# Softmax and relu(h) of a graph network with slice attention worked in their PSUM banks, output stores on ScalarE, attention weights loaded earlier

## What is computed

```python
xn   = layernorm(x)
agg  = segment_sum(xn[src], dst)                     # 6250 x 256
h    = relu(agg @ W_rel + b_rel + xn @ W_root)       # 512 wide
g    = h @ W_ih.T + b_ih + b_hh                      # gates i, g, o are used
c    = sigmoid(i) * tanh(g)
x    = x + (sigmoid(o) * tanh(c)) @ W_fc + b_fc      # called res below

x2   = layernorm(x)
w    = softmax(((x2 @ W_x + b_x) by heads @ W_slice + b_slice) / temperature)   # 8 heads x 64 slices
tok  = (sum over nodes of w * (x2 @ W_fx + b_fx)) / (sum over nodes of w + 1e-5)
q, k, v = tok @ W_q, tok @ W_k, tok @ W_v;  o = softmax(q k^T * scale) v         # 64 slices, 8 heads
out  = x + (w applied to o, heads joined) @ W_out + b_out
```

## Time and profile before

| | us |
|---|---|
| median of 3 runs | 1416.76 (1415.46 to 1417.55) |
| the profiled execution | 1413.04 |
| its span, first to last instruction | 1411.3 |
| PE busy | 1219.1 (86% of the span) |
| PE weight loads, beside PE | 1077.3 (76%) |
| POOL busy | 912.1 (65%) |
| DVE busy | 817.2 (58%) |
| ACT busy | 587.4 (42%) |

### The profile page before, as it was taken

How to read it: one execution, slowest core, us unless ns; L and a number is a source line. 1 busy time by engine, 2 the same in 40 slices (tenths; PEclk the granted TensorE clock), 3 DMA queues, 4 the chain that set the end, 5 groups by cost and what they waited for, 6 DMA issues and landing times.

```text
span 1411.3 us, 26147 instructions
## 1 busy us (share of the span) xinstructions
PE 1219.1 (86%) x8601; PEld 1077.3 (76%) x8601; DVE 817.2 (58%) x2232; ACT 587.4 (42%) x1145; POOL 912.1 (65%) x950
## 2 busy tenths in 40 slices
PE   1315889999999999999999999999999999988995
PEld 0213777888888888888888888878888888887895
DVE  3853345665657655665657655665657656554563
ACT  3631345344434444344434445344434445352231
POOL 1237777777777777777777777777777777500142
PEclk9998999999999999999999999999999999999998
DMA  5755444444444444444444444445444444204495
GB/s 153 226 177 162 119 121 129 139 116 139 125 138 116 137 133 130 138 116 138 125 139 124 130 135 130 138 115 141 124 139 119 133 134 144 86 30 118 154 337 176
DMA packets 118704, 194.82 MB, mean 138 GB/s; under 512 B 49987, under 2 KB 76479, under 8 KB 118652
## 3 DMA queue, kind: packets, MB, share of 16 engines
q0 software_dynamic: 44960, 121.32, 29.9%
q1 hardware_dynamic: 70112, 60.30, 15.1%
q10 hardware_dynamic: 3600, 12.80, 2.3%
HBM read 162.29 MB, written 32.89 MB: 138 GB/s over the span
## 4 chain that ended last, share of the span: by engine, by line
POOL 35%; issue 32%; DMA 18%; PE 9%; SPq 2%; ACT 2%; DVE 1%; POOLq 0%; ACTq 0%; DVEq 0%
POOL ring L576 35%; DMA ring<-table,sidx 14%; PE ps L311 3%; PE ps L313 2%; PE ps L312 2%; DMA table<-ring 2%; ACT ring L646 1%; DMA ring<-dstp 1%; SPq L352 0%; PE ps L975 0%; PE ps L993 0%; DMA ring<-in_b_fx 0%; DMA dstp<-didx 0%; PE ps L1053 0%; DMA swt_d<-swt 0%
## 5 line engine op out<-in xcount | busy, mean ns | idle before, releaser
L576 POOL DMA_INDIRECT ring<-table,sidx x875 | 865.2, 989 | 286.8 <-issue 247.2
L311 PE MATMUL ps<-h_h,wih_h 128*128 128x256 f32 x1200 | 345.9, 288 | 0.5 <-DVE h_l L1341 0.5
L312 PE MATMUL ps<-h_l,wih_h 128*128 128x256 f32 x1200 | 339.2, 283 | 0.0
L313 PE MATMUL ps<-h_h,wih_l 128*128 128x256 f32 x1200 | 339.1, 283 | 0.0
L889 PE MATMUL ps<-ring,oneh 128*125 128x512 f16 x875 | 220.6, 389 | 54.1 <-DMA ring<-table,sidx 53.9
L311 PEld LDWEIGHTS ps<-h_h,wih_h 128*128 128x128 f32 x1200 | 229.6, 191 | 4.0 <-issue 0.9
L312 PEld LDWEIGHTS ps<-h_l,wih_h 128*128 128x128 f32 x1200 | 229.7, 191 | 1.7
L313 PEld LDWEIGHTS ps<-h_h,wih_l 128*128 128x128 f32 x1200 | 229.6, 191 | 0.0
L889 PEld LDWEIGHTS ps<-ring,oneh 128*125 128x125 f16 x875 | 115.6, 139 | 128.5 <-DMA ring<-table,sidx 77.5
L714 ACT ACTIVATE gate<-ps,bgate 128x256 f32<-128x256 f32 x300 | 125.3, 468 | 207.3 <-PE ps L313 207.3
L1257 DVE TENSOR_SCALAR oneh<-iota,rel 128x125 f16<-128x125 f16 x950 | 165.3, 287 | 1.8
(11 more groups left out here) (221 smaller groups left out, 2638.8 us busy)
## 6 DMA issues: line engine op xcount, KB each, us to landing
ring<-table,sidx POOLq DMA_INDIRECT x875, 2.8
swt_d<-swt ACTq DMA_DIRECT2D x25, 500.0 KB
gate<-swt_d SPq DMA_DIRECT2D x19, 500.0 KB, 6.4
ring<-in_x SPq DMA_DIRECT2D x12, 512.0 KB, 5.7
table<-ring SPq DMA_DIRECT2D x12, 512.0 KB, 5.3
xn<-table SPq DMA_DIRECT2D x25, 224.0 KB
xin<-in_x SPq DMA_DIRECT2D x25, 224.0 KB
res<-xin SPq DMA_DIRECT2D x25, 224.0 KB
```

What stands on the lines that cost most here:

```text
L311: eng.matmul(dst, wh, xh, start=first, stop=False)
L312: eng.matmul(dst, wh, xl, start=False, stop=False)
L313: return eng.matmul(dst, wl, xh, start=False, stop=last)
L576: pool.indirect_dma_start(ring[:, e * CH + j, :], None, table, bass.IndirectOffsetOnAxis(ap=sidx[:, e, j:j + 1], axis=0)).then_inc(done, 16)
```

## The change

- `softmax` adds the bias, takes the maximum, subtracts and takes the exponential in the PSUM banks of the logits (`lg`); the multiplication by the inverse sum goes from there into `sw`. The two waits that guard `sw` move down to that multiplication.
- `relu_h` writes its result back into its PSUM bank (`h_bank`); `h_h` and `h_l` are made from there. ACT's wait for the low halves of the cell's result (`hl_lo`) goes.
- `low_x2` and `low_hl` subtract in two instructions of 256 columns in place of one of 512. (`low_h` stays in one piece of 512 for each bank.)
- `f_store` moves from POOL to ACT. In the loop it stands behind the copy `f_high(n, k)` and stores the round before, `f_store(n - 1, k)`; the last five stores come after the last copy.
- The six loads of the attention weights move to the start of SP's turn 25, behind the wait for the last edge sums.
- PE waits for ACT's last copy of transposed weights (`swt_done`) before it transposes the tokens into bank 2.

```diff
@@ SP
+            def load_attention():
+                sp.wait_ge(sum_done[1], NP)
+                sp.dma_start(wfx, a["W_fx"].rearrange("(k p) n -> p k n", p=P)).then_inc(ld_att, 16)
+                sp.dma_start(wout, a["W_out"].rearrange("(h p) n -> p h n", p=D)).then_inc(ld_att, 16)
+                for k, n in enumerate(("W_q", "W_k", "W_v")):
+                    sp.dma_start(wqkv[:, k, :], a[n]).then_inc(ld_att, 16)
+                sp.dma_start(bfx, a["b_fx"].partition_broadcast(G)).then_inc(ld_att, 16)
+
             def turn(t, gather, gnn, ffn, ahead):
+                if isinstance(t, int) and t == NP:
+                    load_attention()
...
             sp.wait_ge(swt_st, 16 * NP)
-            sp.wait_ge(sum_done[1], NP)
...
-            sp.dma_start(bfx, a["b_fx"].partition_broadcast(G)).then_inc(ld_att, 16)
@@
+        def h_bank(q):
+            return ps[:, HA + q, :].rearrange("p (m n) -> p m n", m=2)
@@ POOL
-            def f_store(n, k):
-                p = FB * n + k
-                pool.wait_ge(f_out[k], n + 2)
-                for u, v in PARTS:
-                    pool.dma_start(pair_rows(out, p, C)[u:v], fo[k][u:v]).then_inc(f_st[k], 16)
-            with pool.Fori(0, FN) as n:
-                for k in range(FB):
-                    f_store(n, k)
-            f_store(FN, 0)
-            for k in range(FB):
-                pool.wait_ge(f_st[k], 32 * (FN + (k == 0)))
@@ ACT
             def relu_h(p, q):
-                if q == 0:
-                    after(act, hl_lo, 2 * p)
                 act.wait_ge(h_mm, 2 * p + q + 1)
                 for m in (2 * q, 2 * q + 1):
-                    act.activation(hf[:, m, :], ps[:, HA + q, (m % 2) * 256:(m % 2) * 256 + 256], ACT.Relu,
-                                   bias=brel[:, m:m + 1]).then_inc(h_act, 1)
+                    h = h_bank(q)[:, m % 2, :]
+                    act.activation(h, h, ACT.Relu, bias=brel[:, m:m + 1]).then_inc(h_act, 1)
                 act.wait_ge(h_act, KT * p + 2 * q + 2)
-                act.activation(h_h[:, 2 * q:2 * q + 2, :], hf[:, 2 * q:2 * q + 2, :], ACT.Copy).then_inc(h_hi, 1)
+                act.activation(h_h[:, 2 * q:2 * q + 2, :], h_bank(q), ACT.Copy).then_inc(h_hi, 1)
...
-                        act.activation(sw[0:WN, e, :], sw[0:WN, e, :], ACT.Exp).then_inc(lg_exp, 1)
+                        act.activation(ps[0:WN, XA + e, :], ps[0:WN, XA + e, :], ACT.Exp).then_inc(lg_exp, 1)
...
+            def f_store(n, k):
+                p = FB * n + k
+                act.wait_ge(f_out[k], n + 2)
+                for u, v in PARTS:
+                    act.dma_start(pair_rows(out, p, C)[u:v], fo[k][u:v]).then_inc(f_st[k], 16)
             with act.Fori(1, FN) as n:
                 for k in range(FB):
                     f_high(n, k)
+                    f_store(n - 1, k)
             f_high(FN, 0)
+            for k in range(FB):
+                f_store(FN - 1, k)
+            f_store(FN, 0)
@@ PE
             spin(TOK + 1, 8)
             pe.wait_ge(att_v, V_TOKENS)
+            pe.wait_ge(swt_done, 2 * NP)
@@ DVE
             def low_x2(p):
-                dve.tensor_tensor(x2_l[0:WN, :, :], x2[0:WN, :, :], x2_h[0:WN, :, :].bitcast(F32),
-                                  ALU.subtract).then_inc(x2_lo, 1)
+                for e in range(2):
+                    last = dve.tensor_tensor(x2_l[0:WN, e, :], x2[0:WN, e, :], x2_h[0:WN, e, :].bitcast(F32), ALU.subtract)
+                last.then_inc(x2_lo, 1)
             def low_h(p, q):
-                dve.tensor_tensor(h_l[:, 2 * q:2 * q + 2, :], hf[:, 2 * q:2 * q + 2, :],
+                dve.tensor_tensor(h_l[:, 2 * q:2 * q + 2, :], h_bank(q),
                                   h_h[:, 2 * q:2 * q + 2, :].bitcast(F32), ALU.subtract).then_inc(h_lo, 1)
+            lg = ps[:, XA:XA + 2, :]
             def softmax(p):
                 dve.wait_ge(lg_mm, 2 * p + 2)
-                after(dve, swt_mm, 2 * p)
-                after(dve, sw_hi, p)
-                dve.tensor_tensor(sw[0:WN, :, :], ps[0:WN, XA:XA + 2, :],
-                                  biasx[0:WN, :].unsqueeze(1).to_broadcast([WN, 2, HG]), ALU.add).then_inc(sm_step, 1)
+                dve.tensor_tensor(lg[0:WN], lg[0:WN], biasx[0:WN, :].unsqueeze(1).to_broadcast([WN, 2, HG]),
+                                  ALU.add).then_inc(sm_step, 1)
...
-                dve.tensor_reduce(mx8[0:WN, :], heads(sw), AX.X, ALU.max).then_inc(sm_step, 1)
+                dve.tensor_reduce(mx8[0:WN, :], heads(lg), AX.X, ALU.max).then_inc(sm_step, 1)
...
-                    dve.tensor_tensor(half(sw, e), half(sw, e), of_heads(mx8, e), ALU.subtract).then_inc(lg_sub, 1)
+                    dve.tensor_tensor(half(lg, e), half(lg, e), of_heads(mx8, e), ALU.subtract).then_inc(lg_sub, 1)
             def softmax_end(p):
-                dve.tensor_reduce(sm8[0:WN, :], heads(sw), AX.X, ALU.add).then_inc(sm_step, 1)
+                dve.tensor_reduce(sm8[0:WN, :], heads(lg), AX.X, ALU.add).then_inc(sm_step, 1)
...
+                after(dve, swt_mm, 2 * p)
+                after(dve, sw_hi, p)
                 for e in range(2):
-                    last = dve.tensor_tensor(half(sw, e), half(sw, e), of_heads(rs8, e), ALU.mult)
+                    last = dve.tensor_tensor(half(sw, e), half(lg, e), of_heads(rs8, e), ALU.mult)
...
             def low_hl(p, q):
-                dve.tensor_tensor(hl_l[:, 2 * q:2 * q + 2, :], hf[:, 2 * q:2 * q + 2, :],
-                                  hl_h[:, 2 * q:2 * q + 2, :].bitcast(F32), ALU.subtract).then_inc(hl_lo, 1)
+                for f in (2 * q, 2 * q + 1):
+                    last = dve.tensor_tensor(hl_l[:, f, :], hf[:, f, :], hl_h[:, f, :].bitcast(F32), ALU.subtract)
+                last.then_inc(hl_lo, 1)
```

4 lines of the change are left out of this document (removed).

## The result

The changed kernel takes 1379.28 us (median of 4 runs, 1378.79 to 1381.32), the kernel before beside it 1416.11 (4 runs, 1412.96 to 1417.55). The ratio is 0.9745 with a 95% interval from 0.9729 to 0.9762, so the change brings 36.1 us (0.0255 x 1416). A ratio here is worked out from the fast runs alone and is not the quotient of two medians: on the chips that run the kernel before in some 1415 us the two differ by up to 0.2%, or 3 us. The profiled execution of after took 1378.79 us with a span of 1376.9, against 1413.04 and 1411.3, so the two traces differ by 34.4 us in span.

What follows compares the result with a forecast made beforehand. POOL's gathers, with their issue pauses, were taken to bound the kernel. Loop 22.8, attention weights 2.9 and last stores 0.3, less 0.2 for added pieces, gave 25.8 us: 1416.8 - 25.8 = 1391 us, range 1380 to 1406.

Steps and rivals of the forecast that it cites:

- The last store: At the kernel's end, ACT instead of POOL issues the last pair's two stores: 0.3 us gained.
- The main loop: Turns 1 to 24: fewer gathers stretched by DVE instructions with two SBUF inputs, 0.95 us a turn, 22.8 us (13 to 29).
- k = 15: Gather number 15 of a loop turn, counted from 0: meets the first x_l piece and loses 0.19 us.
- k = 33: Gather number 33 of a loop turn, counted from 0: falls between two norm additions, loses 0 or about 0.65 us.
- the grid: Undisturbed gather starts in a loop turn, one each 1.25 us; DVE instructions met there were to cost 0.6 us a turn.
- rival 6: Slower: loop collisions moved, not removed, 1.9 us a turn against today's 1.55, total 1422 us; chance 0.04.
- PE's wait for rows: In the loop, PE's wait for gathered rows falls from 1.8 to about 0.9 us a turn.
- Attention weights: Before the attention matmuls: loads issued earlier remove PE's wait for them, 2.9 us gained.
- Closing loop: Held by DMA; stores moved to ACT and put off change its time by 0 us (-3 to +5).
- Rival 3: Late stores: closing additions wait for their buffer's store, 0.1 to 0.3 us on some 16 pairs, 1396 us; chance 0.07.
- Work inside PSUM: ACT and DVE writing PSUM: -0.03 to +0.1 us per instruction, taken as 0, covered by POOL in the loop.
- 2 (a better draw): Seam between norm additions met, loop gains 1.2 us a turn, deferred stores help: 1381 us; chance 0.07.

Runs made afterwards that it cites:

- stores alone: Kernel before with only the output stores issued by ACT: 1403.85 us, ratio 0.9905; on the slower chip 1875.47 us, ratio 0.9947.
- the first of the two POOL experiments: Changed kernel, with POOL waiting at its end until ACT's last output stores have landed: 1380.66 us, ratio 0.9751.
- the second: Kernel before, with only the very last pair's output store issued by ACT and POOL not waiting for landings: 1408.41 us, ratio 0.9945.
- the banks alone: Kernel before, with only softmax and relu(h) worked in PSUM, low halves still in one piece: 1397.51 us, ratio 0.9881.
- the experiment alone: Kernel before, with only the six attention loads moved to SP's turn 25 and PE's added wait: 1411.57 us, ratio 0.9972.
- The stores first in line: Changed kernel, with each output store issued ahead of the copy it stood behind in ACT's loop: 1376.04 us, ratio 0.9712.

## Why the prediction was right or wrong

**The last store: this step failed.** The prediction said: "The last pair's two stores take POOL 1.24 us to issue; ACT gives back between nothing and half of it, **0.3**". Measured are 9.9 us, in after, in stores alone (2.79 us behind the last addition) and on the slower chip (2.78). The issue and the landing did shorten a little: from the last addition's end to the landing it was 3.3 us (1398.69 to 1402.0) and is 2.3 (1374.16 to 1376.5). The other 8.9 are POOL's closing drain, which the step did not count, although it stood in the trace before. It falls off the path because POOL is done 170 us earlier. The first of the two POOL experiments shows that the drain comes back once POOL is held to the end, at 4.8 us; the second, that taking one store and the wait from POOL isn't enough. Why a drain behind stores takes 8.9 and one behind gathers 4.8 was not tried.

Without this error the sum would have been 25.8 + 9.6 = 35.4 us, against 36.1 by the ratio and 34.4 between the two traces. That it comes so near is in part luck: the loop was put 1.4 us too high, and the attention weights 1.3 us too low.

**The main loop: right in mechanism and size, with a condition missing.** 22.8 us were forecast, 21.4 came. The mechanism, that only two SBUF inputs hold a gather, is what the traces show: no gather beside a PSUM-reading subtraction is stretched, the mean of 965 is the forecast's "about 965", and the banks alone gave 16.8 us. The rest per turn was forecast at 0.6 us and is 0.7 to 0.9 in turns 7 to 24, for partly other reasons. "k = 15 looks at 607.62, inside the first x_l piece: 0.19" came out at 0.03. "k = 33 looks just where the first norm<-norm,sw gives over to the second: 0, or about 0.65" came out at 0.26, inside the second. And the xin addition, at the start of the turn, was not in the forecast's list of what the grid meets; it costs 0.26. Over turns 1 to 24 the mean is 44.43 us where 45.32 stood, so 0.89 us a turn came instead of 0.95, and that is the 1.4 us that the sum was too high.

Its price for a chance meeting, d x d / 2.5, took all of an instruction's length for d. With the 0.54 and 0.27 us that do hold a gather it is 0.12 and 0.03 us instead of 0.19 and 0.07, and rival 6's count of today's instructions comes to 14 x 0.12 + 8 x 0.03 = 1.9 us a turn, an estimate near the 1.55 seen, where rival 6 had 3.2 and put the rest down to the engines running in step. By the same price rival 6's own sum, 1.9, falls to 14 x 0.03 + 5 x 0.12 = 1.0, where 0.7 to 0.9 are measured.

By the Trainium skill, page "SBUF — State Buffer", section "Who interferes with whom", `tensor_tensor` was not seen to stall DMAs issued by GpSimd. By that sentence the loop would not have moved. Here the measurement decides: 875 gathers, which GpSimd issues, became 24 ns shorter in the mean when tensor-tensor instructions gave up their second SBUF input or were cut, while the one-hots stayed. The other half of what the prediction cites there, a port shared with GpSimd's reads, these traces support.

**PE's wait for rows: wrong, at no cost.** The prediction said it would fall "to about 0.9 us a turn". It went from 39.7 us in 37 waits to 36.0 in 23, which is 1.6 a turn:

```profile
PE ps L888 <- DMA ring<-table,sidx: 36.0, 23, 1.8
```

PE begins each turn at the landing of the last gather and is not done with its work much later than POOL, so I took a shorter turn to eat its wait; but PE got faster too. Its mean clock rose from 0.980 to 0.991, and seven drops of some 3.4 us to half clock, from 272.2 to 1224.5 us, became one, at 1221.4. Between 200 and 1200 us PE is busy for 943.5 us before and 950.0 after, which is 42.7 and 42.3 us a turn; six drops there, 1.7 us lost in each, make 0.5 us a turn over 22 turns, an estimate that fits. Five of these six turns took 45.6 to 45.7 us in place of 45.3, the sixth 45.2. "PE's 43.5 is below the new 44.35 and takes nothing back" held.

**Attention weights: right, with a term left out.** The 2.9 us were found. What the forecast left out is the 1.3 us that the wait cost behind it, through the clock; the experiment alone gave 4.0 (1.6 to 6.4), and its 32 matmuls took 2.0 us.

**Closing loop: right in size, open in detail.** "I take 0 (-3 to +5)" stands against -0.2. That "f_add waits for out_x" was one of the prediction's signs of being wrong, and it did come about. Rival 3's mechanism is there, 14.1 us of waits, and its price is not: rival 3 put 0.1 to 0.3 us on each of some 16 pairs, and the loop is no longer than before. The stores first in line took the waits away and brought 2.4 us in one trace, no more than what separates kernels without such waits. "The closing loop is held by DMA" is not shown either: in the stretch of the earlier trace rows PE is busy for 15.00 of 15.00 us too, and in the kernel before it is busy for 70.7 of the 72 us from 1326 to 1398. Which of the two sets the pace was not tried.

**Work inside PSUM: 0 was taken, and it is a gain.** The exponential takes 582 ns in the bank. The same instruction in SBUF, and the relu, took in the kernel before

```profile
L748 ACT ACTIVATE sw<-sw 125x512 f32<-125x512 f32 x50 | 30.9, 632 | 162.6 <-DVE sw L1368 162.6
...
L698 ACT ACTIVATE hf<-ps,brel 128x256 f32<-128x256 f32 x100 | 41.6, 466 | 105.1 <-PE ps L313 105.1
```

so 50 and 28 ns less, outside the bound of 30 ns at the first (whose input moved to PSUM as well). DVE's addition of the bias takes 1232 ns where it wrote SBUF in 1225: nothing. In the loop POOL covers all of it. The Trainium skill says in "ScalarE: Activation LUTs", section "Step-by-step: what each stage is for", that ScalarE is faster to PSUM than to SBUF, and the relu's rows agree, 438 against 466 ns with only the destination changed.

Of the rivals, 2 (a better draw) came nearest in time, 1381, but for a wrong reason: the seam was not met and the loop gained less than 22.8, not 29. The range's lower end, 1380, is also lower than its own terms give: 1416.8 - 29 - 2.9 - 3 = 1381.9, less a few tenths for PSUM.

## What to carry to other kernels

Before costing what a change does at the end, lay the last piece of the chain against the span: where the chain stops 11 us short, some engine's closing work is the bound, and an engine that issues late work pays for its closing drain in the open. Where one engine's DMA instructions set the pace, look at which instructions of the neighbour they start beside, and which of the two started first. Reading one input from PSUM took the stretch away whole, cutting the instruction in two took most of it, and pieces are the remedy for what has to stay in SBUF. A wait of TensorE costs more than its length if the clock falls behind it.

## What the runs showed of the hardware that was not expected

- GpSimd's closing drain takes 8.9 us where it issued the last output stores (8.892 in seven traces, 9.2 where the very last store was ScalarE's), and 4.8 us behind gathers alone (five traces, and 4.800 where it began 170 us later).
- A DVE instruction with two SBUF inputs holds a gather of GpSimd only if it began before the gather did: none of 521 gathers that met one in its first 0.15 us was stretched, and all of 991 that met one 0.2 us or more after its beginning were.
- A wait of 2.4 to 3.0 us of TensorE brings its granted clock from 2.4 to 1.2 GHz for the work just behind it: 32 small matmuls take 3.0 to 3.7 us (five traces) against 2.0 (five traces).
- One of the chips runs the same kernel in 1890 us instead of 1416, with a mean clock of 0.87 in the trace of stores alone and TensorE idle in front of its matmuls; there the loop's part of the change gave nothing.
